# First dense attention: row maxima of steps 0 and 3 from half the keys' scores plus the positive part of a difference, with ScalarE taking the positive part

## The reference

```
q, k, v = split(x @ qkv_w + qkv_b)          # heads of 8
q, k = rotary(q), rotary(k)
scores = einsum('bhqd,bhkd->bhqk', q, k) * 8 ** -0.5
weights = softmax(scores)                    # subtracts each query's maximum over 1024 keys
attn = einsum('bhqk,bhkd->bhqd', weights, v)
return attn @ out_w + out_b
```

## Time and profile before

| what | us |
|---|---|
| median of 3 runs | 4155.5 (4150.63 to 4158.05) |
| the profiled execution | 4152.44 |
| its span, first to last instruction | 4150.6 |
| the steps of the first dense attention | 424 to 1160 of the span |
| mean granted clock of PE over the span | 0.92 |
| PE, VectorE, ScalarE, GpSimd busy | 3473.8, 2690.9, 2596.3, 1360.0 |

### The profile page before, as it was taken

The page is one execution under the profiler, slowest core; times in us unless marked ns, Lnnn a source line. Parts: engine busy times, 40 slices in busy tenths (PEclk is TensorE's granted clock), DMA queues, the critical chain, the costliest instruction groups (busy, mean ns, idle before and its releaser), DMA issues. The chain is left out here.

```text
span 4150.6 us, 54356 instructions
## 1 busy us (share of the span) xinstructions
PE 3473.8 (84%) x20444; PEld 1530.9 (37%) x20444; DVE 2690.9 (65%) x4473; ACT 2596.3 (63%) x4281; POOL 1360.0 (33%) x1266
## 2 busy tenths in 40 slices
PE   7995888889958898988888799879987899686776
PEld 4672122212221221222222366546655456332333
DVE  5225989989746656565555677557756523568887
ACT  2221676767858989989999587548754332325554
POOL 0501482010011000010000588358840261406886
PEclk9996999999979989999999899989988999897877
DMA  4111131111021001011000111111102012290001
GB/s 141 39 42 45 38 61 29 22 32 17 2 55 26 16 20 27 7 25 16 16 1 1 28 34 35 25 23 34 35 15 86 12 56 56 49 112 6 1 16 26
DMA packets 140860, 137.40 MB, mean 33 GB/s; under 512 B 42632, under 2 KB 105908, under 8 KB 140596
## 3 DMA queue, kind: packets, MB, share of 16 engines
q1 hardware_dynamic: 131060, 116.08, 12.7%
q0 software_dynamic: 8192, 16.79, 1.8%
q10 hardware_dynamic: 1344, 1.05, 0.1%
HBM read 64.12 MB, written 33.82 MB: 24 GB/s over the span
## 5 line engine op out<-in xcount | busy, mean ns | idle before, releaser
L476 PE MATMUL PS<-t 50*128 50x512 bf16 (+2 forms) x3072 | 737.5, 396 | 203.4 <-ACT t L629 55.3
L609 ACT ACTIVATE t<-PS 128x512 f32<-128x512 f32 x1024 | 532.7, 602 | 236.2 <-PE PS L476 235.5
L748 DVE TENSOR_TENSOR t<-t 128x1536 f32<-128x1536 f32 (+1 forms) x384 | 585.1, 1591 | 122.7 <-ACT t L629 70.0
L664 DVE TENSOR_REDUCE t<-PS 128x1 f32<-128x1024 f32 x512 | 600.9, 1215 | 50.7 <-PE PS L468 46.5
L550 PE MATMUL PS<-t 128*9 128x512 f32 x4096 | 550.2, 610 | 12.7 <-DVE t L748 12.3
L476 PEld LDWEIGHTS PS<-t 50*128 50x128 bf16 (+2 forms) x3072 | 158.3, 94 | 985.2 <-ACT t L629 276.9
L631 ACT ACTIVATE t<-PS 128x1536 f32<-128x1536 f32 (+1 forms) x384 | 477.9, 1310 | 54.0 <-PE PS L476 37.1
L629 ACT ACTIVATE t<-PS 128x1536 f32<-128x1536 f32 (+1 forms) x384 | 477.1, 1310 | 34.6 <-PE PS L476 19.4
L468 PE MATMUL PS<-t 48*128 48x512 bf16 x1024 | 342.1, 404 | 45.2 <-DVE t L664 24.7
L1845 POOL TENSOR_TENSOR t<-t 128x512 f32<-128x512 f32 x128 | 159.8, 1270 | 575.8 <-ACT t L1710 575.3
L524 PE MATMUL PS<-t 128*128 128x384 f32 x544 | 269.1, 579 | 0.0
(11 more groups left out here) (413 smaller groups left out, 6329.5 us busy)
## 6 DMA issues: line engine op xcount, KB each, us to landing
t<-scr SPq DMA_DIRECT2D x336, 64.0 KB
t<-t SPq DMA_DIRECT2D x128, 128.0 KB, 2.3
scr<-t SPq DMA_DIRECT2D x96, 128.0 KB, 1.8
t<-t SPq DMA_DIRECT2D x16, 512.0 KB, 13.0
scr<-t SPq DMA_DIRECT2D x2, 2560.0 KB
t<-scr SPq DMA_DIRECT2D x16, 320.0 KB, 3.7
scr<-t SPq DMA_DIRECT2D x16, 320.0 KB, 2.6
t<-scr SPq DMA_DIRECT2D x48, 48.0 KB
```

Of the source, the lines that this page charges most:

```text
L476: return e.op.matmul(PS[:, bk, :], Kx[p // 4 % 2][lo:lo + rows, j, kb * 128:kb * 128 + 128], Qx[p // 4 % 2][lo:lo + rows, j, hf * 512:hf * ...
L609: e.op.activation(P[x % 4][:, 2 * hf + side, :], PS[:, bank((what, p, k, side, hf)), :], ACT.Exp, scale=S8).then_inc(*PW.up((p, k, side, hf)))
L664: e.op.tensor_reduce(MX[p % 2][:, side, qc:qc + 1], PS[:, 2 * side:2 * side + 2, :].rearrange("p a n -> p (a n)"), AX, ALU.max).then_inc(* ...
L748: e.op.tensor_tensor(o, o, SGM[(12 * p + 3 * blk + ti) % 3][:, 0:nu, :], ALU.mult).then_inc(*DG.up((p, blk, ti)))
```

## The change

For pairs 4 to 31 and the query blocks 0 and 3 (`HALVED`), the maximum over 1024 keys is computed in another way. With A the scores of a query with the first 512 keys and B with the second 512, max(A, B) = A + max(B - A, 0), element by element. PE adds a third product per side: the negated queries (`NQ`) times the first half of the keys, accumulated onto the second half's bank, which so holds B - A. ScalarE writes the positive part to SBUF (`RD`), after the two exponentials of a side. VectorE adds A out of PSUM and takes the maximum over the 512 columns in one instruction (`tensor_tensor_reduce`, in the profile two instructions: the operation and a read of its accumulator). GpSimd makes the negated queries once per unit of four pairs, four operations, at step 0 of the unit's predecessor's second pair.

```diff
@@ -303,6 +303,8 @@
                     ML = sb([128, 2, 8], BF16, c)
                     mrow = sb([32, 128], BF16, c)
                     mD = dram([NP, 2, 2, T], BF16)
+                    NQ = [sb([128, 4, 2, 128], BF16, c) for _ in range(2)]
+                    RD = [sb([128, 512], F32, c) for _ in range(2)]
                 else:
                     SGM = [sb([128, 3, 512], F32, c) for _ in range(3)]
                 if mix:
@@ -348,6 +350,8 @@
                             if p % 4 == 0 and k == 0 and p // 4 + 1 < NU:
                                 yield "fetch", p // 4 + 1
                             if first:
+                                if p % 4 == 1 and k == 0 and p // 4 + 1 < NU:
+                                    yield "negate", p // 4 + 1
                                 if k == 1 and p:
                                     yield "evac", p - 1
                                 yield "step", p, k
@@ -408,6 +412,17 @@
                     return 2 <= k <= 4 and (ti == 2 or not taken(p, k - 1)) or (
                         k == 5 and ti < 2 and not taken(p, 4))
 
+                HALVED = (0, 3)
+
+                def halved(p, qc):
+
+                    return p > 3 and qc in HALVED
+
+                def halved_before(p, qc):
+
+                    x = HALVED.index(qc)
+                    return (p, HALVED[x - 1]) if x else (p - 1, HALVED[-1])
+
                 def gated(p, ps):
 
                     return ps != p % 2
@@ -465,9 +480,16 @@
                         if hf == 0:
                             take(e, 2 * side, ("max", p, qc, side), (DV, ("max", p, qc, side)))
                             rows_in(e, p)
+                        less = hf == 1 and halved(p, qc)
                         t = e.op.matmul(PS[:, 2 * side + hf, :],
                                         Qx[p // 4 % 2][lo:lo + KP, j, qc * 128:qc * 128 + 128],
-                                        Kx[p // 4 % 2][lo:lo + KP, j, hf * 512:hf * 512 + 512], start=True, stop=True)
+                                        Kx[p // 4 % 2][lo:lo + KP, j, hf * 512:hf * 512 + 512], start=True,
+                                        stop=not less)
+                        if less:
+                            e.wait_ge(PO, ("negate", p // 4))
+                            t = e.op.matmul(PS[:, 2 * side + 1, :],
+                                            NQ[p // 4 % 2][lo:lo + KP, j, HALVED.index(qc), :],
+                                            Kx[p // 4 % 2][lo:lo + KP, j, 0:512], start=False, stop=True)
                         if hf:
                             t.then_inc(*PM.up(("max", p, qc, side)))
 
@@ -608,6 +630,13 @@
                                     e.wait_ge(SC, (p, k, side, hf))
                                     e.op.activation(P[x % 4][:, 2 * hf + side, :], PS[:, bank((what, p, k, side, hf)), :], ACT.Exp,
                                                     scale=S8).then_inc(*PW.up((p, k, side, hf)))
+                                if mate(p) is not None and halved(mate(p), k):
+                                    m, sd = mate(p), 1 - side
+                                    e.wait_ge(PM, ("max", m, k, sd))
+                                    if (m, k) != (4, HALVED[0]):
+                                        e.wait_ge(DV, ("max", *halved_before(m, k), sd))
+                                    e.op.activation(RD[sd][:], PS[:, 2 * sd + 1, :], ACT.Relu).then_inc(
+                                        *AC.up(("more", m, k, sd)))
                         elif what == "tile":
                             p, ps, blk, ti = i
                             u0, nu = TILES[ti]
@@ -661,6 +690,13 @@
                         e.wait_ge(PM, ("max", p, qc, side))
                         if p > 1:
                             e.wait_ge(DV, ("neg", p - 2))
+                        if halved(p, qc):
+                            e.wait_ge(AC, ("more", p, qc, side))
+                            e.op.tensor_tensor_reduce(
+                                out=RD[side][:], in0=PS[:, 2 * side, :], in1=RD[side][:], scale=1.0, scalar=-3e38,
+                                op0=ALU.add, op1=ALU.max,
+                                accum_out=MX[p % 2][:, side, qc:qc + 1]).then_inc(*DV.up(("max", p, qc, side)))
+                            return
                         e.op.tensor_reduce(MX[p % 2][:, side, qc:qc + 1],
                                            PS[:, 2 * side:2 * side + 2, :].rearrange("p a n -> p (a n)"), AX,
                                            ALU.max).then_inc(*DV.up(("max", p, qc, side)))
@@ -811,6 +847,18 @@
                                 mix.gather(e, RB, ch, PO)
                             if ch > 3:
                                 mix.combine_pool(e, RB, ch - 4)
+                        elif what == "negate":
+                            u, = i
+                            e.wait_ge(HEADS[u % 2], u)
+                            for ch in range(16 * u - 20, 16 * u - 16):
+                                if 0 <= ch < NC:
+                                    e.wait_ge(GR[ch % NR], ch)
+                            for lo in (0, 64):
+                                src = Qx[u % 2][lo:lo + KP, :, :].rearrange("p h (q t) -> p h q t", q=8)
+                                for x, qc in enumerate(HALVED):
+                                    then().tensor_scalar(NQ[u % 2][lo:lo + KP, :, x, :], src[:, :, qc, :], -1.0, None,
+                                                         ALU.mult).then_inc(*PO.up(("negate", u)))
+                            e.wait_ge(PO)
                         elif what == "split":
                             b, qi, hf = i
                             pt = part[hf]
```

More of the change, by code:

```diff
@@ L45 @@
     matmul = transpose = activation = copy = mul = memset = tensor_copy = tensor_scalar = nothing
-    tensor_tensor = scalar_tensor_tensor = tensor_reduce = bn_stats = bn_aggr = reciprocal = nothing
+    tensor_tensor = scalar_tensor_tensor = tensor_reduce = tensor_tensor_reduce = bn_stats = bn_aggr = reciprocal = nothing
     dma_start = indirect_dma_start = nothing
```

## The result

| | before | changed |
|---|---|---|
| median of 4 runs each, us | 4153.07 (4143.53 to 4158.05) | 4207.12 (4200.04 to 4210.07) |
| ratio, 95% interval | | 1.0128 (1.0111 to 1.0145) |
| the profiled execution, its span, us | 4152.44, 4150.6 | 4200.04, 4198.2 |

What follows compares the result with a forecast made beforehand. Plain steps were taken as bound by a PE and ScalarE loop, with VectorE deciding at two places per pair. 4152.4 + 66.5 (25 pairs at 2.66 us) + 3.1 to the median = 4222 us; range 4180 to 4255.

Steps and rivals of the forecast that it cites:

- VectorE is not the limit of a plain step: Plain steps follow a 2.44 us loop through PE and ScalarE; VectorE's two reductions take 2.38 us.
- the 23 us of the earlier trace: PE's waits for L742 and L766 together, the most a faster VectorE could give back at these places.
- The new wait ends 1.39 us late at step 0 and 1.27 us at step 3: VectorE waits for the second Relu: L729 moves from +2.58 to +3.97, the reciprocal from +2.70 to +3.97; 2.66 us per pair.
- The halved maximum at 0.83 us: VectorE's operation plus accumulator read, replacing a 1.19 us reduction; lower bound 0.77, upper bound 1.30.
- The rival of half rate: VectorE's halved maximum takes 1.30 instead of 0.83 us: 23.5 us more, 4246 us; chance 13%.
- ScalarE's pass at 0.49 us: Each halved maximum adds one ScalarE pass over 128x512 from PSUM, 55 us more work for 112, no table load.
- ScalarE's own delay of step 1: Step 1's exponentials come at 3.43 instead of 2.57, 0.86 us, lying beside VectorE's delay.
- The rival that this delay and PE's are all of the cost: VectorE catches up; only 0.86 + 0.22 = 1.08 us per pair remain, 27 us, 4183 us; chance 13%.
- 28 pairs, three of them absorbed: 28 pairs at 2.66 us, less pairs 4, 12 and 20 where other stalls hide it: 25 x 2.66 = 66.5 us.
- The three stalls for SP's queue: In pairs 4, 12 and 20 ScalarE stands 9.54, 3.55 and 4.94 us behind row loads; 2.66 us disappear each time.
- Negations at nothing: GpSimd's negations, about 2.5 us per unit, hidden by idle time; late ones would cost 17 us, 4239 us, chance 3%.
- The other signs: PE's waits for L742's and L766's counterparts in all pairs; steps 1 to 3, 3 to 5 longer; 4 to 7 still 2.44 us apart.

Runs made afterwards that it cites:

- short_maxima_only: Changed kernel with VectorE's short maxima over a tile of zeros, no positive parts or third products; 4298.52 us, 0.9999 of the kernel before.
- step0_only: Changed kernel with only query block 0 halved (56 maxima); 4326.1 us, 1.0065 of the kernel before.
- step3_only: Changed kernel with only query block 3 halved (56 maxima); 4334.89 us, 1.0078 of the kernel before.
- passes_only: Changed kernel with ScalarE's extra passes over SBUF data nobody waits for, old reductions, no third products; 4312.77 us, 1.0044 of the kernel before.
- negations_only: Kernel before plus GpSimd's negations, nothing else of the change; 4301.07 us, 1.0002 of the kernel before.
- relu_two_earlier: Changed kernel with positive parts behind the first and second exponential of a halved step; 4307.8 us, 1.0022 of the kernel before.
- sums_before_fourth: Kernel before with weighted sums between third and fourth score, last maxima product behind the fourth; 4259.6 us, 1.0249 of the kernel before.

## Why the prediction was right, and where its sizes were off

The forecast was +66.5 us, 4222; measured were +47.6 us between the profiled executions and +54 by the medians, 4207, inside the range. The mechanism held; the size was 12 to 19 us too large. Step by step:

- **VectorE is not the limit of a plain step.** Right: in `short_maxima_only` VectorE's work is shorter without a new wait, and the pair goes only from 20.45 to 20.29 us. My remark that the 23 us of the earlier trace rows are the most that could come back was true as a bound and far too high as a hope: PE's transposes bind just behind.
- **The new wait ends 1.39 us late at step 0 and 1.27 us at step 3.** Right: L765 at +3.92 (forecast 3.97), the reciprocal at +3.99 (3.97); by themselves the two places cost 1.34 and 1.25 us. The moved positive parts show that the wait is on ScalarE's order; `step0_only` and `step3_only`, that the two add.
- **The halved maximum at 0.83 us.** The lower of my two bounds held. Groups of the changed kernel, 424 to 1210:

```profile
L695 DVE CUSTOM_DVE_ANT_0 t<-PS,t 128x512 f32<-128x512 f32 x112 | 77.4, 691 | 124.3 <-ACT t L638 98.9 <-PE PS L484 20.0 <-PE PS L490 5.2
...
L638 ACT ACTIVATE t<-PS 128x512 f32<-128x512 f32 x112 | 70.0, 625 | 0.0
...
L859 POOL TENSOR_SCALAR t<-t 48x512 bf16<-48x512 bf16 x28 | 41.6, 1486 | 305.1 <-DMA t<-scr 302.5 <-DMA t<-scr,t 0.9
...
L695 DVE DVE_READ_ACCUMULATOR2_ANT t<- 128x1 f32 x112 | 9.3, 83 | 0.0
```

  0.69 + 0.08 = 0.77: the second arithmetic operation costs nothing over the addition of the earlier trace rows. A plain pair costs 2.58 instead of 2.66 us; at step 0 the shorter operation is the difference (3.92 for 3.97). The rival of half rate is refuted: 691 ns for 128x512 is what a plain addition of that shape takes (686). The rule of the Trainium skill (Vector Engine (DVE) Microarchitecture Reference, Points that are easy to get wrong) names two SBUF sources; here one is in PSUM, so what happens with two was not tried.
- **ScalarE's pass at 0.49 us.** Right: 1121.47 to 1121.94 is 0.47, 0.61 to 0.65 us each, and no table load. ScalarE's own delay of step 1 is 0.86 us in `passes_only`, as forecast (+3.43 against +2.57), and 0.77 in the changed kernel (+3.34). The rival that this delay and PE's are all of the cost is refuted by the 2.58 us; `passes_only` prices ScalarE's share of it, 0.74 us per pair, where the rival had 0.86 (its other 0.22 was PE's third product, which that run does not have).
- **28 pairs, three of them absorbed.** This is the term that was mis-sized, by 16 of the 19 us. I took every pair for a plain one, and the one execution of each kernel that was profiled has its own chances.
  - In step 0 of pairs 9, 17 and 25 VectorE is already late, by statistics and additions of the output's projection. In the changed kernel it idles 0.46 and 0.40 us in pair 17 (0.09 and 0.77 in the other two) instead of 1.61 and 0.77, because it comes later than in a plain pair and the positive parts don't. The intervals that follow, of pairs 10, 18 and 26, grew by 1.01, 1.02 and 1.24 us, 3.3 together, where 3 x 2.66 = 8.0 was forecast: 4.7 us. Timeline of VectorE in the changed kernel at such a step 0 (ScalarE's first exponential at 850.74):

```profile
851.09 1.28 DVE L957 BATCH_NORM_STATS2 t<-t 128x6 f32<-128x128 f32 x4
...
852.83 0.69 DVE L695 CUSTOM_DVE_ANT_0 t<-PS,t 128x512 f32<-128x512 f32 x1 [0.46 <-ACT t L638]
...
854.66 0.18 DVE L765 TENSOR_SCALAR t<-t 128x16 f32<-128x16 f32 x1
```

  L765 starts at +3.92 as elsewhere, but in the kernel before L729 stood at 829.25, +3.91 after 825.34, since its statistics (825.68) came there too. At this place the halved step 0 costs nothing; what the interval grew by is about step 3's share.
  - The intervals of pairs 12 and 20 grew by only 0.85 and 0.79 us, 1.6 together, where 5.3 was forecast: 3.7 us. Here VectorE is not late in the kernel before (L729 at +2.67 in step 0 of pairs 11 and 19). Most of it is PE's clock in the profiled execution before: from 694.1 to 697.5 and from 881.8 to 885.2 the granted clock was 0.5, the 1.2 GHz level, after PE had stood still 0.72 us for L742, and then the full level again. In the first stretch:

```profile
693.76 1.62 PE L550 MATMUL PS<-t 128*9 128x512 f32 x8
...
695.31 2.08 PE L484 MATMUL PS<-t 128*128 128x512 f32 x2
```

  The same products take 1.05 and 1.12 us in the changed kernel (from 709.98), whose clock stayed at full level after the same 0.72 us. In `negations_only` the interval of pair 12, at full clock, is 23.89 us instead of 25.44, and that of pair 20, with the same drop, 25.47. So about 3.1 of these 3.7 us are no property of the change.
  - The three stalls for SP's queue absorbed more than their own pair's 2.66 us: the intervals of pairs 5, 13 and 21 got shorter by 3.88, 0.43 and 3.07 us, 7.4 together, where I had put zero. ScalarE's stall at pair 4, in the changed kernel:

```profile
549.23 1.08 ACT L631 ACTIVATE t<-PS 128x512 f32<-128x512 f32 x2 [3.97 <-PE PS L498]
```

  It was 9.54 us. I had reasoned that the row loads wait for GpSimd's splits of the pair before and so move as that pair does. But in the kernel before these splits waited for GpSimd itself, which was at its gathers until 514.91; in the changed kernel GpSimd idles 2.02 us for VectorE at 517.74, and the loads start at 526.43, 2.2 us later than 524.19, while the pair is 6.7 us later. What set their time was mostly GpSimd's work, and that had not moved.
  The 3.07 us of pair 21 are another matter. The row loads and the store of the maxima stand nearly where they stood, as seen from the pair, but the reload came 6.8 us after the store instead of 10.9. In the other traces this wait at pair 20 lies anywhere from 5.7 to 14.9 us; in `negations_only` it is 6.4, and the interval of pair 21 is 20.46 us there instead of 26.10. So this gain is luck of the profiled execution.
  The remaining intervals came to 50.1 us where 20 x 2.66 = 53.2 was forecast; 1.6 of these 3.1 us are the 0.08 us per pair, the rest I did not follow. The sum: 66.5 - 4.7 - 3.7 - 7.4 - 3.1 = 47.6 us, as measured. Without the two clock drops and pair 21's short reload, 6.2 us together, it would be about 54 us, an estimate that agrees with the medians.
- **Negations at nothing.** Right in what they cost, wrong in what they last: 1.49 us each and not 0.62. Their cover held. `negations_only` has 1.0002.
- **The other signs.** PE's waits grew at both counterparts, steps 1 to 3 and 3 to 5 are longer, and steps 5 to 6 (1136.23 to 1138.66) are still 2.43 us apart, as forecast.

Not settled: what makes the maxima's store and its reload lie 5.7 us apart in one execution and 14.9 in another. At pair 4 it is 11.6 us before and 11.9 changed, so it does not disturb the comparison there.

## What to carry to other kernels

- Before moving work from a busy engine to one with idle time, find the instruction that ends the chain and ask when its operand can be there. Here 55 us less work on VectorE cost 48 to 54 us, because its operand stood behind two exponentials in an in-order queue; moving it up by one place won back 1.0, by another 0.6 us of 2.6.
- An engine's gaps are not slack if they are inside a loop: ScalarE's 0.37 us gaps per step are its wait for PE, which waits for ScalarE.
- Multiply a per-pair cost only by the pairs that look like the one it was read from; go through the intervals for those in which the engine is late anyway, and for stalls ask whose work sets their end. Before a difference of one interval is explained, compare that interval in traces where nothing about it was changed.

## What was new about the hardware

- GpSimd's negation of 48x512 bf16 takes 1.49 us, where its cast of 128x512 to bf16 takes 0.62. The operand here is four strided pieces of 128; whether the stride or the operation costs was not tried.
- `tensor_tensor_reduce` with one operand in PSUM takes 691 ns for 128x512, as fast as a plain addition (686), and 83 ns for its accumulator.
- In the kernel before, a VectorE instruction on 128x16 that takes 0.17 us elsewhere takes 1.07 us when it starts while GpSimd is at a TENSOR_TENSOR on SBUF, in pairs 11 and 19 alike; it ends when GpSimd's does:

```profile
688.75 1.15 POOL L834 TENSOR_TENSOR t<-t 128x512 f32<-128x512 f32 x1
...
688.86 1.07 DVE L729 TENSOR_SCALAR t<-t 128x16 f32<-128x16 f32 x1
```

- The store of the maxima and the reload that waits for it lie 10.9 us apart in the kernel before at pair 20 (L885 at 911.56, L892 at 922.44) and 6.8 us apart in the changed kernel (L933 at 941.83, L940 at 948.65), in the timeline of SP's queue; over all traces kept, from 5.7 (`relu_two_earlier`) to 14.9 us (`sums_before_fourth`).
- The granted clock of PE fell to the 1.2 GHz level for 3.4 us in the middle of the stage in some executions and not in others at the same place, which alone lengthened a pair by about 1.55 us (25.44 against 23.89 us at pair 12).
